# The last layer's attention core rewritten: tiles of 128, 128 and 17 rows instead of three of 91, three pairs of PSUM banks shared by both kinds of scores, products with the values in one run per four heads

## The reference

```python
q = (x @ Wq + bq).reshape(B, S, H, Dh)      # B 32, S 273, H 16, Dh 16
k = (x @ Wk + bk).reshape(B, S, H, Dh)
v = (x @ Wv + bv).reshape(B, S, H, Dh)
scores = jnp.einsum('bqhd,bkhd->bhqk', q, k) / jnp.sqrt(jnp.float32(Dh))
attn = jax.nn.softmax(scores, axis=-1)
ctx = jnp.einsum('bhqk,bkhd->bqhd', attn, v).reshape(B, S, D)
attn_out = ctx @ Wo + bo
```

## Time and profile before

| | us |
|---|---|
| median of 3 runs | 5672.37 (5671.71 to 5673.27) |
| the profiled execution, its own time | 5665.37 |
| its span in the trace | 5663.7 |
| stage e, from its first instruction to its last store | 3988.7 to 4926.5 |
| granted clock over the whole span | 0.856 |

### The profile page before, as it was taken

The page is one execution under the profiler, slowest core; times in us unless marked ns, Lnnn a source line. Parts: engine busy times, 40 slices in busy tenths (PEclk is TensorE's granted clock), DMA queues, the critical chain, the costliest instruction groups (busy, mean ns, idle before and its releaser), DMA issues. The chain is left out here.

```text
span 5663.7 us, 99769 instructions
## 1 busy us (share of the span) xinstructions
PE 4386.4 (77%) x26575; PEld 2865.2 (51%) x26575; DVE 3787.5 (67%) x9299; ACT 2479.5 (44%) x5698; POOL 594.0 (10%) x928
## 2 busy tenths in 40 slices
PE   6999788400289886777788776787799898799998
PEld 5777566300155554555555554555455555454554
DVE  4555333588788787777667774555777777567777
ACT  1222333575333333677777773222466666510110
POOL 0111000000000001000000001111111111122221
PEclk9999899755689998677777878888799999899999
DMA  2222233589744443322222223555333333311111
GB/s 82 74 75 70 97 138 138 187 253 356 276 132 122 126 133 87 80 69 71 72 72 72 72 67 99 155 157 151 96 90 91 89 90 94 89 45 50 53 53 34
DMA packets 380379, 616.99 MB, mean 109 GB/s; under 512 B 43574, under 2 KB 310388, under 8 KB 380276
## 3 DMA queue, kind: packets, MB, share of 16 engines
q1 hardware_dynamic: 367956, 614.35, 36.5%
q0 software_dynamic: 12320, 1.40, 0.2%
HBM read 345.02 MB, written 269.21 MB: 108 GB/s over the span
## 5 line engine op out<-in xcount | busy, mean ns | idle before, releaser
L1670 DVE TENSOR_REDUCE e_neg<-ps 91x1 f32<-91x273 f32 x1536 | 571.8, 427 | 137.0 <-PE ps L1491 129.6
L1603 ACT ACTIVATE e_probT<-ps 91x273 f32<-91x273 f32 x1536 | 491.6, 392 | 291.3 <-PE ps L1491 290.5
L1218 PE MATMUL ps<-k_downT,f_o 128*91 128x256 f32 x1152 | 260.8, 386 | 456.7 <-DVE f_o L1126 456.6
L2346 PE MATMUL ps<-m_we,m_xT 128*128 128x512 f32 x1104 | 505.6, 602 | 0.0
L1218 PEld LDWEIGHTS ps<-k_downT,f_o 128*91 128x91 f32 x1152 | 183.4, 161 | 525.8 <-issue 457.7
L1489 PE MATMUL ps<-c_mask_kq,c_identb 91*91 91x91 bf16 x1536 | 323.4, 241 | 105.6 <-ACT g_probT L1603 73.2
L1491 PE MATMUL ps<-e_k,e_q 96*91 96x273 bf16 x1536 | 344.0, 306 | 62.6 <-DMA e_k<-s_parts 27.9
L1491 PE MATMUL ps<-g_q,g_k 102*91 102x273 bf16 (+5 forms) x1536 | 328.2, 294 | 50.0 <-DVEq L1676 49.2
L2281 DVE SCALAR_TENSOR_TENSOR m_acc<-ps,m_weight,m_acc 128x256 f32<-128x256 f32 x552 | 257.4, 480 | 117.5 <-PE ps L2346 103.9
L1491 PE MATMUL ps<-e_q,e_k 128*91 128x273 bf16 x1536 | 285.6, 290 | 39.3 <-DMA e_q<-e_shift 37.4
L2346 PEld LDWEIGHTS ps<-m_we,m_xT 128*128 128x128 f32 x1104 | 203.1, 192 | 212.0 <-issue 194.8
(11 more groups left out here) (306 smaller groups left out, 9694.1 us busy)
## 6 DMA issues: line engine op xcount, KB each, us to landing
s_gate<-b_gu SPq DMA_DIRECT2D x32, 819.0 KB, 4.6
s_up<-b_gu SPq DMA_DIRECT2D x32, 819.0 KB, 6.1
c_g<-s_gate SPq DMA_DIRECT2D x32, 819.0 KB, 7.2
s_gated<-c_g SPq DMA_DIRECT2D x32, 819.0 KB, 8.7
d_g<-s_gated SPq DMA_DIRECT2D x32, 819.0 KB, 10.2
d_u<-s_up SPq DMA_DIRECT2D x32, 819.0 KB, 10.4
s_o<-d_o SPq DMA_DIRECT2D x32, 819.0 KB
f_o<-s_o SPq DMA_DIRECT2D x32, 819.0 KB, 4.4
```

Of the source, the lines that this page charges most:

```text
L1218: last = nc.tensor.matmul(ps[0:R, t // 2, (t % 2) * D:(t % 2 + 1) * D], o[:, u, k, t * R:(t + 1) * R], downT[:, k, :], start=(k == 0), sto ...
L1603: nc.scalar.activation(probT[0:R, p % 8, b, :], src, ACT.Exp, scale=float(HD) ** 0.5 if kinds[h] == COS else 1.0)\
L1670: last = nc.vector.tensor_reduce(neg[:, u, t, h:h + 1], src, AX.X, ALU.max, negate=True)
L2346: last = nc.tensor.matmul(ps[0:R, EBANK[m % 4], :], xT[:, u, k, t * R:(t + 1) * R], we[:, k, 2 * p:2 * p + 2, :].rearrange("p e d -> p (e ...
```

## The change

The core of the last layer becomes a function of its own, `attention_full`. T is cut into 128, 128 and 17 rows (`KEYS`). The two full tiles of a head go side by side into a pair of banks and are read by one instruction of 546 columns. The 17 rows left of four heads go to the four 32-column tiles of the array into one bank, 32 partitions apart, and are read by one instruction (`look_rest`, `main_rest`). Looks and main passes share three pairs of banks (`PAIR`) in turn. The product of four heads is issued in one run of three key tiles behind the fourth head of the next four. Two shifts of 8 heads stand in the place of three. `q` and `k` stay bf16, and `probT` and the values f32.

`phase_g1` stores the values by rows of tokens ([NB, T, 512]) in two DMAs instead of one, and cuts their matmuls and additions into 128, 128 and 17 rows.

The diff, cut to its core:

```diff
+KEYS = (128, 128, REST)
...
+def attention_full(nc, c, ps, NB, parts_dram, v_dram, ctx_dram):
...
+        PAIR = ((0, 2), (2, 4), (4, 6))
+        SUM, TURNED = 6, 7
...
+        @block.sync
+        def _(sp):
...
+            def batch(i, u, before, more):
+                n, at = 2 * i + u, (i, u)
+                if before and more:
+                    sp.wait_ge(S["pv"].sem, S["pv"].at((i, u - 1)))
+                    sp.sem_inc(passed, 1)
+                    load_v(n + 1, 1 - u)
+                if more:
+                    sp.wait_ge(S["s"].sem, S["s"].at(at, 2 * UNITS))
...
+            sp.wait_ge(ones_set, 1)
+            sp.wait_ge(cleared, 5)
...
+        @block.gpsimd
+        def _(pool):
...
+            nc.gpsimd.memset(vrest[:], 0.0).then_inc(cleared, 1)
+            pool.wait_ge(cleared, 5)
+            nc.gpsimd.memset(k[96:128], 1.0).then_inc(ones_set, 1)
...
+        @block.tensor
+        def _(pe):
...
+            def turn(n, u, p):
+                pe.wait_ge(S["spread"].sem, S["spread"].at(n, p + 1))
+                pe.wait_ge(S["out"].sem, S["out"].at(n, -1) if p else S["out"].at((n[0], n[1] - 1), 1))
...
+            def body(i, b, posts=True, mains=True, pres=True):
...
+                for g in range(GROUPS):
+                    y, h = UNITS * g, 4 * g
...
+                    if mains and g % 2 == 0:
+                        pe.wait_ge(laid[u][g // 2], LAID * (mi + 1))
...
+                    if pres:
+                        looked(y - 1)
+                        look(tu, h, PAIR[0][0])
+                    if mains:
+                        emptied(y - 1)
+                        main(u, h, PAIR[1][0])
+                    if g >= 2 and mains:
+                        turn_back(now, u, g - 2, (then, 1) if g == 3 and pres else None)
...
+                    if pres:
+                        looked(y)
+                        emptied(y)
+                        look(tu, h + 1, PAIR[2][0])
+                    if mains:
+                        if pres:
+                            looked(y + 1)
+                        emptied(y)
+                        main(u, h + 1, PAIR[0][0])
+                    if g == 0 and mains:
+                        turn(now, u, 1)
+                    if g == 2 and pres:
+                        turn(then, tu, 0)
...
+                        main(u, h + 2, PAIR[2][0])
...
+                        look(tu, h + 3, PAIR[0][0])
...
+                        main(u, h + 3, PAIR[1][0])
+                    for t in range(NT):
+                        if g >= 1 and mains:
+                            combine(now, u, mi, g - 1, t)
...
+                        look_rest(tu, g, PAIR[2][0])
+                    if mains:
+                        main_rest(u, g, PAIR[2][0] + 1)
...
+        @block.vector
+        def _(dve):
...
+            nc.vector.memset(q[96:128], 0.0).then_inc(cleared, 1)
+            nc.vector.memset(oT[:], 1.0).then_inc(cleared, 1)
+            nc.vector.memset(probT[:], 0.0).then_inc(cleared, 1)
+            nc.vector.memset(probR[:], 0.0).then_inc(cleared, 1)
...
+            def largest(n, u, g, a, bank):
+                dve.wait_ge(S["look"].sem, S["look"].at(n, UNITS * g + a + 1))
+                nc.vector.tensor_reduce(neg[:, u, g // 2, :, 4 * (g % 2) + a], ps[:, bank:bank + 2, 0:T], AX.X, ALU.max,
+                                        negate=True).then_inc(S["looked"].sem, 1)
...
-                sp.dma_start(v_dram[batch_of(n)], vp[:, u].rearrange("p t h w -> p (t h w)")).then_inc(v_stored[u], 16)
+                sp.dma_start(v_dram[batch_of(n), 0:WHOLE].rearrange("(t p) w -> p t w", p=128),
...
-        run(attention_core, c, ps, NB, "e", [SDPA] * H, False, HD, parts2, v2, ctx2)
+        run(attention_full, c, ps, NB, parts2, v2, ctx2)
```

More of the change, by code:

```diff
@@ L886 @@
 RP = 128
+GROUPS = H // 4
+WHOLE = 256
+REST = T - WHOLE
+KEYS = (128, 128, REST)
 def pipeline(eng, NB, stages):
@@ L1750, in phase_g1 @@
         bqk = sb("bqk", [128, 2, CT])
-        projb, bv = sb("projb", [R, D]), sb("bv", [R, D])
+        projb, bv = sb("projb", [R, D]), sb("bv", [128, D])
         cx = sb("cx", [R, 2, NT, D])
@@ L1813, in store_v @@
                 sp.sem_inc(passed, 1)
-                sp.dma_start(v_dram[batch_of(n)], vp[:, u].rearrange("p t h w -> p (t h w)")).then_inc(v_stored[u], 16)
+                sp.dma_start(v_dram[batch_of(n), 0:WHOLE].rearrange("(t p) w -> p t w", p=128),
+                             vp[:, u, 0:2].rearrange("p t h w -> p t (h w)")).then_inc(v_stored[u], 16)
+                sp.dma_start(v_dram[batch_of(n), WHOLE:T], vp[0:REST, u, 2].rearrange("p h w -> p (h w)"))\
+                    .then_inc(v_stored[u], 16)
             def store_parts(n, u, i):
@@ L1831, in _ @@
             sp.dma_start(projb[:], row(projb_dram).broadcast_to([R, D])).then_inc(w_loaded, 16)
-            sp.dma_start(bv[:], row(bv_dram).broadcast_to([R, D])).then_inc(w_loaded, 16)
+            sp.dma_start(bv[:], row(bv_dram).broadcast_to([128, D])).then_inc(w_loaded, 16)
             for u in range(2):
@@ L1837, in _ @@
             for u in range(2):
-                for s, times in ((h_stored, 1), (x_stored, 1), (p_stored, 2 * CT), (v_stored, 1)):
+                for s, times in ((h_stored, 1), (x_stored, 1), (p_stored, 2 * CT), (v_stored, 2)):
                     sp.wait_ge(s[u], 16 * times * (NB // 2))
@@ L1918, in values @@
                 dve.wait_ge(S["v"].sem, S["v"].at(n))
-                dve.wait_ge(v_stored[u], 16 * i)
-                bias = bv[:].rearrange("p (h w) -> p h w", w=HD)
+                dve.wait_ge(v_stored[u], 32 * i)
                 for t in range(NT):
-                    x = ps[0:R, 6 + t // 2, (t % 2) * D:(t % 2 + 1) * D].rearrange("p (h w) -> p h w", w=HD)
-                    last = nc.vector.tensor_tensor(vp[:, u, t, :, 0:HD], x, bias, ALU.add)
+                    rows = KEYS[t]
+                    x = ps[0:rows, 6 + t // 2, (t % 2) * D:(t % 2 + 1) * D].rearrange("p (h w) -> p h w", w=HD)
+                    last = nc.vector.tensor_tensor(vp[0:rows, u, t, :, 0:HD], x,
+                                                   bv[0:rows].rearrange("p (h w) -> p h w", w=HD), ALU.add)
                 last.then_inc(S["v_out"].sem, 1)
@@ L1975, in values @@
                     for k in range(CT):
-                        last = nc.tensor.matmul(ps[0:R, 6 + t // 2, (t % 2) * D:(t % 2 + 1) * D],
-                                                xT[:, u, k, t * R:(t + 1) * R], wv[:, k, :],
+                        last = nc.tensor.matmul(ps[0:KEYS[t], 6 + t // 2, (t % 2) * D:(t % 2 + 1) * D],
+                                                xT[:, u, k, t * 128:t * 128 + KEYS[t]], wv[:, k, :],
                                                 start=(k == 0), stop=(k == CT - 1))
@@ L2387, in program @@
     parts2 = scratch("parts2", [NB, 2, PARTS, HD * H, T], BF16)
-    v1, v2 = (scratch(n, [NB, R, NT * H * VW]) for n in ("v1", "v2"))
+    v1, v2 = scratch("v1", [NB, R, NT * H * VW]), scratch("v2", [NB, T, H * VW])
     ctx = ExitStack()
```

341 lines of the change are left out of this document (340 added, 1 removed).

## The result

The changed kernel takes 5503.07 us (median of 4 runs, 5499.27 to 5505.89), the kernel before 5672.04 us beside it (4 runs, 5660.65 to 5673.27). The ratio is 0.9706, with a 95% interval from 0.9689 to 0.9723: about 169 us faster. The profiled execution took 5503.66 us. Forecast was 5539 us, with a range of 5490 to 5635.

What follows compares the result with a forecast made beforehand. TensorE was taken to bound stage e, with waits for maxima and shift rows on top. Stage e -143.3 us, start +11.8 and -2.1, `phase_g1` nothing: -133.6, so 5531.8 us profiled, 5539 us median, range 5490 to 5635.

Steps and rivals of the forecast that it cites:

- What bounds the kernel, prices: Stage e: TensorE sets most steps; maximum of 546 columns 0.72 us alone, exponential 0.615, set of rests 0.12.
- The ring paces, TensorE and VectorE are not full: Stage e: three pairs of banks pace a group until the product; VectorE needs 3.8 of 5.7 us, TensorE about 4.4.
- A group's schedule: Stage e, four heads: 5.60 us with a shift, 5.61 behind it, taken as 5.75; a batch 22.7 against 27.63.
- The 0.1 us for a second wait: Stage e, main pass: a second wait with an address computed behind the first adds 0.1 us, estimated between 0 and 0.12.
- Shift rows: Stage e, group behind a shift: rows used 4.83 us after the shift's last step, so 5.75 us was taken.
- The rival with late rows: Stage e: shift rows take 6.36 us, every second group lasts 7.13; +86 us, 5625 us; chance 0.11.
- The clock: Stage e: granted clock 0.95, a tenth of the time at 1.2 GHz, making a batch 23.45 us instead of 22.7.
- Late transfers: Stage e: twice a batch took 33.3 instead of 27.6 us before; 11.4 us left in the sum.
- The start: Start of stage e: clearing delays loads, +11.8 us; from first look to first main pass -2.1 us.
- `phase_g1` at nothing: Stage ahead of stage e: passes keep number and columns, one more DMA issue per batch is off the path; 0 us.
- the bound of 11 us: `phase_g1`: one more DMA issue per batch, at most 32 x 0.35 = 11 us if it were on the path.
- the likeliest case: Whole kernel: the forecast of 5539 us, with its own range of 5510 to 5575 us; chance 0.55.

Runs made afterwards that it cites:

- the kernel with half maxima: Changed kernel with each head's maximum in stage e over the first 136 of 273 columns of both tiles: 5446.81 us, ratio 0.9610.
- the kernel with three places: Changed kernel with the product's three sets apart, behind the second, third and fourth head of a group, instead of in one run: 5463.53 us, ratio 0.9640.

## Why the prediction was right in sign and 36 us too high

- **What bounds the kernel, prices.** Right. Maximum 719 ns (0.72), exponential 627 (0.615), rests 0.12 us a set, TensorE on within 0.06 us.
- **The ring paces, TensorE and VectorE are not full.** Right: idle time before main passes, and the kernel with half maxima shows that their length is on the path. What made the batch shorter is the work: 6.1 us less of it a batch, with 0.3 us more of waits.
- **A group's schedule.** 5.60 worked out for a group with a shift, 5.55 measured (4382.21 to 4387.76). 5.61 for the one behind it, 5.37 measured: the fourth main pass starts 3.26 us in, not 3.39, the product 0.34 behind that (0.36 reckoned), and product and rests take 1.77 us instead of 1.86. The 0.1 us for a second wait was nothing at the first place where it could be seen. Both kinds of group together were put 0.58 us a batch too long, 18 us in all.
- **Shift rows.** A wait that did not come: 5.61 was raised to 5.75 with 4.83 us from one row, where the rows now take 4.00 and are awaited once in 500 us. 0.28 us a batch, 9 us in all. The rival with late rows had only the start's 6 us for it.
- **The clock.** 0.95 was taken, 1.00 granted: (23.45 - 22.7) x 31 = 23 us too much, the largest term on that side. In the changed kernel and all twelve experiments the middle of the stage stood at 0.99 or 1.00, with TensorE busy 86% to 97%. The Trainium skill, "TensorE: Matmul & The Clock Gate", in its section on a second failure mode by PSUM queue cycling, tells of a kernel with 512 columns whose clock swings between both levels as it goes round the banks. This ring does not bear that out: it goes round three pairs of banks with halts of 0.26 to 0.52 us and stays at 2.4 GHz.
- **Late transfers.** 11.4 us were left in; one batch was late, by 1.7 us. In the kernel with three places four half batches were, by 9 us in all. It was right to put it into the sum, but it falls as it falls.
- **The start.** +11.8 and -2.1 forecast, +9.6 and +0.6 measured: 0.5 us off in sum.
- **`phase_g1` at nothing.** Wrong by 25 us, and wrong in kind: the bound of 11 us was for a DMA issue, which two kernels showed to be free. "Passes keep their number and columns" was true and didn't help, since it is the granted clock over them that changed.

The sum for the profiled execution, what was too much counted as positive: 757.2 - 699.3 = 58 us too much for the stage behind its first main pass (31 x (23.45 - 21.85) = 50, late transfers 10, less 2), less 25 for `phase_g1`, less some 5 elsewhere. So -161.7 (5503.7 against 5665.4) for -133.6, 28 us apart. The other 8 of the 36 us are the 7.0 carried over to the median: the profiled execution before was 7 us faster than its median, the one after 0.6 us slower. The misses partly cancelled, 58 us one way and 30 the other, and that is luck: the time fell in the range, but under the likeliest case's own 5510.

Not seen before the run, and worth 29 us in its stage: the change's run of three sets. The prediction counted that maxima of the fourth head hide behind it, but not that the same sets would have hidden two waits within the group. A batch has gone from 27.63 to 21.85 us in spite of the run. How much of that is the cut's fewer passes, the fewer changes of tiling or the ring, no run shows apart; of the wide maximum alone it is known (16 to 20 us).

## What to carry to other kernels

Where TensorE waits in several places for an answer, work that depends on nothing goes in pieces in front of those waits, even if a piece costs a change of tiling; a run of it at the end leaves them open. Look first at which waits there are: a piece in front of no wait only costs (0.08 us here), and a piece in front of the first of two may only move the wait on to the second. Read a stage that was "only recut" too: if its batches alternate between a low and a high clock, a few tenths of a microsecond of work can cost one a batch, and the place to look is the clock over the first set of a batch, not its instruction count. And when an engine's clearing waits for another's, check whether both are needed at all.

## What the runs showed of the hardware

- The granted clock and a loop of batches can lock, as in `phase_g1`. With tiles of 91 rows a batch takes 16.15 us with 12 matmuls in the values' set and 17.05 with 13; in the second, the batches come 17.00 and 17.13 us apart in turn, and each starts on a low stretch that covers most of the set. The Trainium skill, "TensorE: Matmul & The Clock Gate", in its section on HAM oscillation, tells of a loop that begins each pass at the low clock because of a wait for DMA. The traces agree as to the loop, with another wait: 3.3 us for VectorE. In these runs one matmul a batch makes it jump by 0.9 us.
- One maximum of 546 columns takes 719 ns, one exponential 627 ns; two maxima of 273 in their place take 0.06 us more a head, and the batch of 16 heads grew by 0.64 us, 0.04 a head.
- VectorE and GpSimd clearing SBUF side by side (7.34 and 7.37 us for 32 partitions of 8736 bf16) took what they took one after the other (7.34 and 7.38).
